# Layer 1 of a four-layer sequence model on one core: the input stage worked by halves of the sequence

## What is computed

```python
h = layernorm(x) * (1 + scale) + shift          # scale, shift, gate come from c
h = h[:, perm]                                  # a gather of rows
xz = h @ W_in                                   # 256 -> 1024
xm, z = split(xz, 2)                            # 512 and 512
xm = silu(causal_conv_4_taps(xm) + conv_b)      # called u in the kernel
dtr, Bm, Cm = split(xm @ W_xp, [64, 80])        # the "x projection", 512 -> 96
dt = softplus(dtr @ W_dt + b_dt)                # 64 -> 512
# scan over 1024 steps, state 512 x 16:
#   hst = hst * exp(dt * A) + (dt * xm) * Bm ;  y = sum(hst * Cm)
y = (y + xm * D_param) * silu(z)
out = x + gate * (y @ W_out)[:, inv_perm]
```

## Time and profile before

| | us |
|---|---|
| median of 3 runs | 1943.45 |
| lowest and highest | 1943.37, 1945.23 |
| profiled execution, its own time | 1945.84 |
| span of the profiled execution | 1943.5 |
| of this: TensorE busy | 1845.3 |
| VectorE busy | 1600.7 |
| ScalarE busy | 1425.8 |
| GpSimd busy | 1048.6 |

### The profile page before, as it was taken

One profiled execution on the slowest core, in us unless ns is written; L12 is line 12 of the kernel. 1 busy time (PEld: TensorE's weight loads), 2 busy tenths in 40 slices (PEclk: granted clock), 3 DMA queues, 4 the chain that ended last, 5 costly groups with the idle time before them and its releaser, 6 DMA issues.

```text
span 1943.5 us, 32682 instructions
## 1 busy us (share of the span) xinstructions
PE 1845.3 (95%) x12312; PEld 1337.9 (69%) x12312; DVE 1600.7 (82%) x2125; ACT 1425.8 (73%) x2661; POOL 1048.6 (54%) x603
## 2 busy tenths in 40 slices
PE   6989899999999999999999999999998999999997
PEld 3664899948998599969995799689974333332323
DVE  5565899768998699989995999889987999999742
ACT  3426899468993899799974999799954377777775
POOL 3031599526994299939980699479944400003000
PEclk9989899998999999999999999999999799999999
DMA  5023111021111111101110121021101111111000
GB/s 202 1 85 99 59 57 55 32 72 43 56 59 37 51 54 60 51 24 55 56 44 2 40 60 56 24 72 58 58 15 32 38 42 38 37 37 36 17 23 22
DMA packets 57547, 95.18 MB, mean 49 GB/s; under 512 B 14951, under 2 KB 23559, under 8 KB 55982
## 3 DMA queue, kind: packets, MB, share of 16 engines
q1 hardware_dynamic: 55854, 88.90, 15.2%
q0 software_dynamic: 1536, 4.20, 0.7%
HBM read 73.55 MB, written 6.91 MB: 41 GB/s over the span
## 4 chain that ended last, share of the span: by engine, by line
PE 63%; POOL 14%; ACT 8%; DVE 8%; issue 6%; DMA 1%; SPq 1%; DVEq 0%; ACTq 0%; POOLq 0%
POOL A L1019 13%; PE PS L865 10%; PE PS L840 10%; PE PS L256 8%; PE PS L1603 6%; PE PS L1556 6%; PE PS L1763 5%; PE PS L846 5%; PE PS L265 3%; DVE A L1569 2%; PE PS L441 2%; PE PS L872 1%; ACT A L931 1%; ACT A L908 1%; PE PS L243 1%
## 5 line engine op out<-in xcount | busy, mean ns | idle before, releaser
L1019 POOL TENSOR_TENSOR A<-A 128x1024 f32<-128x1024 f32 x384 | 897.6, 2396 | 223.2 <-ACT small L923 111.0
L931 ACT ACTIVATE A<-A,negA 128x512 f32<-128x512 f32 x768 | 547.3, 715 | 34.0 <-DVE A L1000 24.4
L1000 DVE TENSOR_TENSOR_SCAN A<-A,PS 128x512 f32<-128x512 f32 x384 | 436.2, 1201 | 44.8 <-PE PS L846 23.8
L1000 DVE TENSOR_TENSOR_SCAN A<-A,small,PS 128x512 f32<-128x512 f32 x384 | 451.2, 1259 | 5.3 <-ACT A L931 5.3
L865 PE MATMUL PS<-ident,A 128*128 128x128 f32 x3072 | 408.5, 276 | 20.4 <-ACT A L737 13.3
L840 PE MATMUL PS<-A 128*128 128x128 f32 x3072 | 393.8, 276 | 0.9 <-ACT A L915 0.6
L865 PEld LDWEIGHTS PS<-ident,A 128*128 128x128 f32 x3072 | 352.3, 143 | 30.0 <-ACT A L737 15.9
L840 PEld LDWEIGHTS PS<-A 128*128 128x128 f32 x3072 | 368.1, 192 | 2.3 <-DVE A L1000 2.0
L1569 DVE TENSOR_REDUCE A<-PS 128x1 f32<-128x512 f32 x512 | 319.3, 681 | 38.9 <-PE PS L1556 37.3
L1800 ACT ACTIVATE A<-PS 128x512 f32<-128x512 f32 x512 | 267.2, 603 | 101.9 <-PE PS L1763 101.6
L908 ACT ACTIVATE A<-A,small 128x512 f32<-128x512 f32 x320 | 228.6, 714 | 17.3 <-PE PS L846 16.8
(11 more groups left out here) (194 smaller groups left out, 1842.7 us busy)
## 6 DMA issues: line engine op xcount, KB each, us to landing
A<-scrc SPq DMA_DIRECT2D x192, 256.0 KB, 3.1
A<-A SPq DMA_DIRECT2D x360, 32.0 KB
scr<-A SPq DMA_DIRECT2D x4, 1024.0 KB, 4.8
W<-in_wa SPq DMA_DIRECT2D x2, 1536.0 KB, 9.7
X<-in_x SPq DMA_DIRECT2D x4, 512.0 KB, 5.3
scr<-W SPq DMA_DIRECT2D x128, 1.5 KB
out<-X SPq DMA_DIRECT2D x4, 512.0 KB, 2.9
W<-in_w SPq DMA_DIRECT2D x1, 1984.0 KB, 7.3
```

Of the source, the lines that this page charges most:

```text
L931: e.activation(A_B[i % 4], r.DT[:, dt, ci * 512:(ci + 1) * 512], ACT.Exp, scale=negA[:, r.n, dt * 16 + s:dt * 16 + s + 1]).then_inc(*decay ...
L1000: e.tensor_tensor_scan(h, a, u, init, ALU.mult, ALU.add).then_inc(*scanned.up((q, i)))
L1019: e.tensor_tensor(h, h, CB[k % 2].unsqueeze(1).broadcast_to([128, 2, 512]), ALU.mult).then_inc(*weighed.up((q, pair)))
```

## The change

TensorE now turns, projects and so on by halves: the two transposed banks of half 0, its four `xm` products, then the same for half 1, then the four `z` products of half 0, then the x projection of half 0, then the four `z` products of half 1, and only then the first `dt` products. ScalarE follows that order: it scales a half, copies its four `xm`, and takes u and gates in pairs of 128x512, where u had been made of whole tiles of 1024. VectorE convolves eight tiles of 512 steps in the place of four of 1024. For b = 1 `add_first` stands ahead of `inputs_v`, where it had stood between the first half's maximum and its sum.

```diff
                 banks.seek(0)
-                turn_t(e, w, "ht", lambda i, h: XR[:, i, h * 128:(h + 1) * 128], (2 * b, 2 * b + 1), lambda i: None)
-                w.wait_ge(*transfer("w1").at(0))
-                for m in range(4):
-                    for c in range(2):
-                        w.wait_ge(*act.at(("ht", 2 * b + c, 1)))
+                for c in range(2):
+                    turn_t(e, w, "ht", lambda i, h: XR[:, i, h * 128:(h + 1) * 128], (2 * b + c,), lambda i: None)
+                    w.wait_ge(*transfer("w1").at(0))
+                    w.wait_ge(*act.at(("ht", 2 * b + c, 1)))
+                    for m in range(4):
                         project_t(e, w, ("xm", b, m, c), lambda k, m: W_in[:, k, m * 128:(m + 1) * 128], 2, m, lambda k: HT[:, k, c * 512:(c + 1) * 512])
-                for m in range(4):
-                    for c in range(2):
+
+                def gate_in(c, tiles):
+                    for m in tiles:
                         project_t(e, w, ("z", b, m, c), lambda k, m: W_in[:, k, 512 + m * 128:640 + m * 128], 2, m, lambda k: HT[:, k, c * 512:(c + 1) * 512])
-                inputs_t(e, w, r, lambda c: w.wait_ge(*act.at(("u", b, 3))), lambda part: fuse_t(e, w, b) if part == 2 else None)
+
+                gate_in(0, range(4))
+                banks.seek(0)
+
+                def between(part):
+                    if part == 0:
+                        gate_in(1, range(4))
+                    if part == 2:
+                        fuse_t(e, w, b)
+
+                inputs_t(e, w, r, lambda c: w.wait_ge(*act.at(("u", b, 3, c))), between)
...
-                turn_s(e, w, "ht", lambda h, c: HT[:, h, (c % 2) * 512:(c % 2 + 1) * 512], (2 * b, 2 * b + 1), ACT.Identity,
-                       lambda h, b: GH[:, 1, 0, h, b:b + 1], lambda h, b: GH[:, 1, 1, h, b:b + 1])
                 if b:
                     w.wait_ge(*pe.at(("yg", 0, 6)))
-                for m in range(4):
-                    for c in range(2):
+                for c in range(2):
+                    turn_s(e, w, "ht", lambda h, c: HT[:, h, (c % 2) * 512:(c % 2 + 1) * 512], (2 * b + c,), ACT.Identity,
+                           lambda h, b: GH[:, 1, 0, h, b:b + 1], lambda h, b: GH[:, 1, 1, h, b:b + 1])
+                    for m in range(4):
                         w.wait_ge(*pe.at(("xm", b, m, c)))
...
-                for m, gates in enumerate(((), (0, 1), (2,), (3, 4, 5, 6, 7))):
-                    w.wait_ge(*dve.at(("conv", b, m)))
-                    e.activation(r.U[:, m, :], ACC[:, m, :], ACT.Silu, bias=col("l1cb", m)).then_inc(*act.up(("u", b, m)))
-                    for i in gates:
...
-                w.wait_ge(*transfer("mods_out").at(0))
-                inputs_s(e, w, r, lambda part: None)
+
+                def gate_in(c, m):
+                    w.wait_ge(*pe.at(("z", b, m, c)))
+                    e.activation(ZT[:, m, c * 512:(c + 1) * 512], bank(("z", b, m, c)), ACT.Silu).then_inc(*act.up(("z", b)))
+                    banks.give(("z", b, m, c), act.now())
+
+                for m in range(4):
+                    w.wait_ge(*dve.at(("conv", b, m, 0)))
+                    e.activation(r.U[:, m, 0:512], ACC[:, m, 0:512], ACT.Silu, bias=col("l1cb", m)).then_inc(*act.up(("u", b, m, 0)))
+                    gate_in(0, m)
+
+                def between(part):
+                    if part == 0:
+                        for m in range(4):
+                            w.wait_ge(*dve.at(("conv", b, m, 1)))
+                            e.activation(r.U[:, m, 512:S], ACC[:, m, 512:S], ACT.Silu, bias=col("l1cb", m)).then_inc(*act.up(("u", b, m, 1)))
+                            gate_in(1, m)
+                        w.wait_ge(*transfer("mods_out").at(0))
+
+                inputs_s(e, w, r, between)
...
-                for m in range(4):
-                    w.wait_ge(*act.at(("xm", b, m, 1)))
-                    e.tensor_scalar(ACC[:, m, :], XM[:, m, 0:S], col("l1cw", 4 * m), None, ALU.mult).then_inc(*dve.up())
-                    for j in range(1, 4):
-                        w.wait_ge(*dve.now())
-                        e.scalar_tensor_tensor(out=ACC[:, m, :], in0=XM[:, m, j:j + S], scalar=col("l1cw", 4 * m + j), in1=ACC[:, m, :],
-                                               op0=ALU.mult, op1=ALU.add).then_inc(*dve.up(("conv", b, m)))
+                for c in range(2):
+                    for m in range(4):
+                        o = ACC[:, m, c * 512:(c + 1) * 512]
+                        w.wait_ge(*act.at(("xm", b, m, c)))
+                        e.tensor_scalar(o, XM[:, m, c * 512:(c + 1) * 512], col("l1cw", 4 * m), None, ALU.mult).then_inc(*dve.up())
+                        for j in range(1, 4):
+                            w.wait_ge(*dve.now())
+                            e.scalar_tensor_tensor(out=o, in0=XM[:, m, c * 512 + j:(c + 1) * 512 + j], scalar=col("l1cw", 4 * m + j), in1=o,
+                                                   op0=ALU.mult, op1=ALU.add).then_inc(*dve.up(("conv", b, m, c)))
...
-                inputs_v(e, w, r, add_first if b else None, lambda: fuse_v(e, w, b))
+                if b:
+                    add_first()
+                inputs_v(e, w, r, None, lambda: fuse_v(e, w, b))
```

## The result

The changed kernel is slower: 1952.87 us median (1946.47 to 1956.96, 13 runs) against 1945.23 us (1942.31 to 1947.77, 13 runs), a ratio of 1.0037 with a 95% interval of 1.0029 to 1.0045, some 7 us. The forecast was + 2.4 us, "same", with 1949.3 us as the upper end of the range. The traces shown here come from single runs: the first one of the changed kernel is its slowest run, 1956.96 us.

What follows compares the result with a forecast made beforehand. TensorE's 36 back-to-back products, then ScalarE's table load, were taken to bound the stage. b = 0: + 2.0 - 0.6 - 0.4 = + 1.0 us; b = 1: + 2.0 - 0.6 = + 1.4; 1943.45 + 2.4 = 1945.85 us, range 1942.5 to 1949.3.

Steps and rivals of the forecast that it cites:

- Behind the products: From the last product to ScalarE's Abs: 1.92 us in place of 2.54, a gain of 0.6 us per batch element.
- Between the products: Ahead of half 1's first `xm` product: TensorE waits for ScalarE's scalings, a loss of 2.0 us per batch element.
- In front of the products: Start of b = 0: products start 0.8 us earlier at half clock, a gain of 0.4 us, b = 0 only.
- The clock's places as a rival of 0.19: TensorE's half-clock stretches around the stage's end and scan start grow: slower, 1947.6 to 1949.3 us; chance 0.19.
- the 2.4 of the sum: Whole kernel: + 1.0 us for b = 0 and + 1.4 us for b = 1, together + 2.4 us, 0.12% more.
- The wait of 2.0 us ahead of the second `dt` group: TensorE stands 2.0 us for ScalarE's copy, where it stood 1.3; a clock fall might follow.
- The convolution by halves: VectorE's eight tiles take 2.75 us each, hidden, no cost; the rival that they set the end, 1962 us, has 0.04.
- `add_first`: VectorE: 5.7 us moved ahead of the first maximum, into idle time after the convolution; no gain.
- u in pieces: ScalarE makes u in eight pieces of 0.6 us instead of four of 1.15: 0.2 us more, within idle time.
- The idle time of TensorE really filled: Rival: all four 1.3 us waits ahead of `dt` groups go, faster, 1938.2 us; chance 0.04.
- The first `dt` wait: TensorE ahead of the first `dt` products: at most 0.1 us idle, where it waited some 1.3 us.

Runs made afterwards that it cites:

- the transposes in front: Changed kernel, but TensorE turns both halves ahead of the first input product and ScalarE scales all four banks ahead of its first copy; 1946.73 us, ratio 1.0012.
- the x projection is put back: Changed kernel, but with all eight gate products ahead of the first x projection, on TensorE and ScalarE; 1951.08 us, ratio 1.0032.
- The filler ahead of it: Changed kernel with 40 unused 128x128 matmuls on TensorE while it waits for the gather ahead of b = 0; 1951.05 us, ratio 1.0031.
- the one on the thin products: Changed kernel with both halves turned first, 24 and 8 unused matmuls in two TensorE waits, and fuse_t's two-column products between its wide ones; 1958.59 us, ratio 1.0068.
- the kernel before with the filler: Kernel before the change with 40 unused 128x128 matmuls on TensorE ahead of b = 0; 1945.73 us, ratio 1.0009.
- the kernel with the transposes in front and the second filler: Changed kernel with both halves turned first and 8 unused matmuls in TensorE's wait ahead of the second step-size products; 1946.84 us, ratio 1.0008.

## Why the prediction was wrong, step by step

- **Behind the products, - 0.6 us each: right.** 1.93 us from the last gate to Abs, and 0.55 us gained in the chain with the transposes in front, 0.61 lost when the x projection is put back.
- **Between the products, + 2.0 us each: right, a little small.** The hand-over took 2.01 us. But 7.15 + 24.32 us are 31.47: the two pieces together take 0.29 us more than the single one of 31.18, and I had no term for that. So b = 1 lost 1.75 us, where I had 1.4.
- **In front of the products, - 0.4 us for b = 0: wrong, and this is the first step that failed.** I took the clock's rise at 151.2 us as a fixed time and let the earlier start run against it. It is no fixed time: with the stop of 0.96 us after eight transposes the clock rose 6.7 to 8.7 us after the first transpose (five traces), and without it after 2.7 to 5.5 us (five traces, two of them of the changed kernel with the transposes in front). The stage of b = 0 lost 3.5 us instead of 1.0. The filler ahead of it shows the cause: at the full clock the changed kernel's stage takes 37.69 us, and then b = 0 and b = 1 cost the same. So of the 3.5 us, 1.6 are the schedule's at the full clock (37.69 less 36.06) and 1.9 the clock's, where I had put - 0.4.
- **The clock's places as a rival of 0.19: the second failure.** I saw that the two batch elements had the same total at half the clock, took that for a sign that the total doesn't move, and gave the rival less than a fifth. It came: of the 8.0 us, 2.7 lie in scan starts and scans whose instructions nobody touched, 2.0 of them for b = 1. There the clock is at 0.50 for 13.7 us in all three traces of after, and for 10.2, 10.2 and 6.8 us in those of before: the fall lasts 10.2 us in the first two, and in the third one more lies at the longer wait ahead of the second `dt`. The equal totals were an accident of my one trace: in the second and third trace of before, the total for b = 0 is 6.8 us, not 10.2. And for b = 1 the fall of the earlier trace rows begins 0.5 us behind the thin products, not while they run. The 8.0 us are the 2.4 of the sum, 2.5 more for b = 0, 0.35 more for b = 1 and this 2.7, but all of these are read from the same traces, so that they add up confirms nothing.
- **The wait of 2.0 us ahead of the second `dt` group** came as worked (1.93 to 1.94 us), and so did its effect in kind, in 3 of 10 batch elements.
- **The convolution by halves, `add_first`, u in pieces: right.** 2.76 us for a tile against 2.75, nobody waits, and the pieces show no term for them. A half-width u took 0.71 us, not 0.6, and no wait for it is seen.
- **The idle time of TensorE really filled: it was not.** The first `dt` wait vanished as forecast, the second grew, and Abs follows the last gate.

What stays open is the cause of the 2.7 us. That the clock falls at the scan's start at another point of the work than before is seen (17.6 us behind Abs of b = 1 in the first trace, where it was 19.3), but no experiment moved that point alone, since the one on the thin products failed for its bank. Nor do three traces of each kernel suffice: in that of the kernel before with the filler, where b = 1 has the code of the kernel before, this part of b = 1 takes 183.25 us, as long as after the change, and with 10.2 us at half the clock. That something beyond the input stages is lost is seen from the runs, though: these stages give 5.2 us, and the interval of the ratio starts at 5.6. Also, the kernel with the transposes in front and the second filler should have come out at 1944 and measured 1946.8, with an interval that reaches to 0.9996; whether that is scatter, the runs don't settle. Its trace doesn't help, since it is that of the second fastest of its 12 runs (1940.46 us, of 1940.39 to 1951.24).

## What to carry to other kernels

A rearrangement that lets one engine hand over to another in the middle of a dense row of matmuls pays the hand-over, a little for the restart of the row (0.29 us here), and, if it lies near the row's start, a later rise of TensorE's clock; moving a cheap step (here 0.96 us of transposes) out of a wait's shadow is a loss even where no instruction is added. The rise and the falls of the clock depend on the schedule and also move from one execution to the next, so a sum of terms should carry them as terms wherever the rows show 0.50 near the edit, and take the length of a stretch from more than one trace. Idle time of TensorE that no work can fill may be worth filling with matmuls whose results nobody reads, provided that they end before the wait does; here 40 of them ran over it in both traces, and 24 in one of two.

## What the runs showed of the hardware that I had not expected

- The same transposes and products, with the granted clock at 0.50 when they began, ran at half the clock for 2.7 to 5.5 us when TensorE went on without a stop, and for 6.7 to 8.7 us when it stopped for 0.96 us after 1.97 us of work (five traces of each kind). The changed kernel's stage of b = 0 was 2.5 to 3.4 us longer for it than at the full clock (40.17 and 41.09 against 37.69 us).
- Matmuls of the identity with itself, 128x128, kept the clock at 1.00 through a wait in which it otherwise fell: it fell in all ten traces without them and in none of the four with them.
- A wait of 1.93 us in otherwise dense work was followed by a fall in three of ten cases, one of 1.3 us in none of ten, one of 4.61 us in both cases seen.
